# Rounding in three VectorE operations instead of four, before a bf16 product and before a transpose

## The reference

```python
def _layernorm(x, axis=-1, eps=1e-5):
    ...
    return (x - m) / jnp.sqrt(v + eps)

def _act_quant(x):
    scale = 127.0 / jnp.clip(jnp.max(jnp.abs(x), axis=-1, keepdims=True), 1e-05)
    xq = jnp.clip(jnp.round(x * scale), -128.0, 127.0) / scale
    return x + jax.lax.stop_gradient(xq - x)
def _bitlinear(x, w):
    return jnp.einsum('bsi,oi->bso', _act_quant(x), _weight_quant(w))

# feed-forward: HIDDEN = 1024, INNER = 4096
gate = jax.nn.silu(_bitlinear(x, w_gate))
up = _bitlinear(x, w_up)
return _bitlinear(gate * up, w_down)

# the layer
x = x + attention(_layernorm(x), ...)
x = x + feed_forward(_layernorm(x), w_gate, w_up, w_down)
```

## Time and profile before

| what | us |
|---|---|
| median of 2 runs | 8739.44 |
| lowest and highest run | 8737.64, 8741.25 |
| the profiled execution, its own time | 8731.81 |
| its span on core 1, the slowest | 8730.3 |
| spans of the 8 cores | 8703.8 to 8730.3 |
| VectorE busy | 5261.6 (60%) |
| TensorE busy | 4117.8 (47%) |
| ScalarE busy | 1586.2 (18%) |

### The profile page before, as it was taken

How to read it: one execution, slowest core, us unless ns; L and a number is a source line. 1 busy time by engine, 2 the same in 40 slices (tenths; PEclk the granted TensorE clock), 3 DMA queues, 4 the chain that set the end, 5 groups by cost and what they waited for, 6 DMA issues and landing times.

```text
span 8730.3 us, 121031 instructions; the slowest of 8 cores (8703.8 to 8730.3 us)
## 1 busy us (share of the span) xinstructions
PE 4117.8 (47%) x38438; PEld 2587.6 (30%) x38438; DVE 5261.6 (60%) x12636; ACT 1586.2 (18%) x2602; POOL 60.4 (1%) x102
## 2 busy tenths in 40 slices
PE   0015545555555546645455454555344353353453
PEld 0015522222222225522233232223233232232232
DVE  5666667777677666667677676664544435435434
ACT  0000023333333320013233232331000000000000
POOL 0000000000000000000000000000000000000000
PEclk9997778888888887778788787886666666565566
DMA  8641000000000001100000000002333333343343
GB/s 279 227 137 35 30 4 1 4 1 4 1 1 1 1 18 35 37 7 1 4 1 1 4 1 1 1 1 61 65 82 80 75 87 63 68 93 64 75 87 68
DMA packets 835921, 394.33 MB, mean 45 GB/s; under 512 B 803427, under 2 KB 803555, under 8 KB 829156
## 3 DMA queue, kind: packets, MB, share of 16 engines
q1 hardware_dynamic: 827044, 353.00, 17.1%
q0 software_dynamic: 8256, 33.58, 0.9%
HBM read 352.95 MB, written 33.55 MB: 44 GB/s over the span
## 4 chain that ended last, share of the span: by engine, by line
DVE 47%; PE 26%; issue 11%; DMA 7%; DVEq 7%; ACT 1%; SPq 0%; ACTq 0%; POOLq 0%; POOL 0%
DVE w_lo L771 15%; DVE w_hi L769 9%; PE pb_av L454 6%; PE pf_u L1189 2%; PE pf_d L1361 2%; PE pf_g L1184 2%; PE pf_d L1189 2%; PE pf_d L1184 2%; DMA f_wd<-wdq 2%; PE pb_s L736 2%; DVE ln_lo L471 2%; DVE ln_hi L469 2%; PE pb_o L840 1%; DVE f_guq L1334 1%; PE pb_q L840 1%
## 5 line engine op out<-in xcount | busy, mean ns | idle before, releaser
L759 ACT ACTIVATE w<-pb_s,cbias 128x512 f32<-128x512 f32 x2048 | 1297.4, 684 | 1532.9 <-PE pb_s L736 1519.9
L771 DVE TENSOR_TENSOR w_lo<-w,w_hi 128x512 bf16<-128x512 f32 x2048 | 1416.8, 692 | 159.1 <-issue 6.8
L769 DVE CAST w_hi<-w 128x512 bf16<-128x512 f32 x2048 | 874.8, 427 | 563.8 <-issue 357.1
L712 PE MATMUL pb_av<-vA,w_hi 128*128 128x129 bf16 x4096 | 516.5, 226 | 1142.3 <-DVEq L774 1142.1
L712 PEld LDWEIGHTS pb_av<-vA,w_hi 128*128 128x128 bf16 x4096 | 383.5, 100 | 1642.7 <-issue 1642.7
L1361 PE MATMUL pf_d<-f_guq,f_wd 128*128 128x256 bf16 x2048 | 291.9, 315 | 667.0 <-DVE f_guq L1334 560.6
L712 PE MATMUL pb_av<-vB,w_hi 128*128 128x129 bf16 x4096 | 517.1, 226 | 0.0
L736 PE MATMUL pb_s<-q_hi,h_hi 64*128 64x512 bf16 x2048 | 463.3, 412 | 102.7 <-ACT w L759 71.7
L716 PE MATMUL pb_av<-vA,w_lo 128*128 128x65 bf16 x4096 | 491.1, 198 | 0.0
L716 PE MATMUL pb_av<-vB,w_lo 128*128 128x65 bf16 x4096 | 489.4, 198 | 0.0
L736 PE MATMUL pb_s<-q_lo,h_hi 64*128 64x512 bf16 x2048 | 458.6, 407 | 0.0
(11 more groups left out here) (220 smaller groups left out, 6856.8 us busy)
## 6 DMA issues: line engine op xcount, KB each, us to landing
f_wg<-wgq SPq DMA_DIRECT2D x256, 256.0 KB, 3.2
f_wu<-wuq SPq DMA_DIRECT2D x256, 256.0 KB, 3.7
f_wd<-wdq SPq DMA_DIRECT2D x64, 1024.0 KB, 8.4
wraw<-wgT SPq DMA_DIRECT2D x16, 2048.0 KB, 10.2
wraw<-wuT SPq DMA_DIRECT2D x16, 2048.0 KB, 9.9
wraw<-wdT SPq DMA_DIRECT2D x64, 512.0 KB, 4.5
xa<-x_full SPq DMA_DIRECT2D x64, 512.0 KB, 3.5
x_tm<-x_full SPq DMA_DIRECT2D x16, 512.0 KB, 13.5
```

What stands on the lines that cost most here:

```text
L712: te.matmul(pav[:, pofs:pofs + 129], w_hi[:, wofs + st * 128:wofs + (st + 1) * 128], vb[:, rc * 132:rc * 132 + 129], start=(rc == 0 and st ...
L759: a_e.inc(sc.activation(w32[:, slot:slot + 512], pb_s[hidx][:, 0:512], AFT.Exp, bias=cbias[:, hidx:hidx + 1], scale=1.0 / 64))
L769: v.tensor_copy(w_hi[:, slot:slot + 512], w32[:, slot:slot + 512])
L771: v.tensor_tensor(w_lo[:, slot:slot + 512], w32[:, slot:slot + 512], w_hi[:, slot:slot + 512], ALU.subtract)
```

## The change

The result t g + (u + v) becomes u h + v with h = g + 1, kept in a new tensor `h_t` of one fp32 value per partition. Where g is 0, h is 1 and the result is u + v. Where g is -1, h is 0 and the result is v. This takes the addition and the DRAIN behind it out of both quantizations, and the last operation reads `f_u` and `f_v` (or `f_si` and `f_fb`) in place of `f_t` and `f_u` (or `f_gr` and `f_si`). At the start, one DRAIN and one 128x1 operation are added, and the semaphore `s_g` is raised by the new operation. `h_t` is declared before all large buffers but `x_tm`, so that what is declared behind it starts 32 bytes later.

```diff
--- before.py
+++ after.py
@@ -92,6 +92,7 @@
     onesb = sb("onesbs", [1, 128], BF16)
     eps_t = sb("eps_t", [128, 1], F32)
     g_t = sb("g_t", [128, 1], F32)
+    h_t = sb("h_t", [128, 1], F32)
     sc_t = sb("sc_t", [128, 8], F32)
     mkrow = sb("mkrow", [1, 32], F32)
     mh_row = sb("mh_row", [1, 512], F32)
@@ -147,7 +148,9 @@
         v.drain()
         v.tensor_sub(sc_t[:, 2:3], sc_t[:, 1:2], sc_t[:, 0:1])
         v.drain()
-        s_g.inc(v.tensor_scalar(g_t[:], sc_t[:, 2:3], 4.0, -1.0, ALU.mult, ALU.add))
+        v.tensor_scalar(g_t[:], sc_t[:, 2:3], 4.0, -1.0, ALU.mult, ALU.add)
+        v.drain()
+        s_g.inc(v.tensor_single_scalar(h_t[:], g_t[:], 1.0, ALU.add))
 
     with ExitStack() as wes:
         wsb = lambda n, s, d: wes.enter_context(nc.sbuf_tensor(n, s, d))
@@ -1071,10 +1074,8 @@
                     v.tensor_scalar(f_u[:], f_t[:], M23, -M23, ALU.add, ALU.add)
                     v.tensor_scalar(f_v[:], f_t[:], M52, -M52, ALU.add, ALU.add)
                     v.drain()
-                    v.tensor_add(f_u[:], f_u[:], f_v[:])
-                    v.drain()
                     v.scalar_tensor_tensor(f_xq[:, st2 * E:(st2 + 1) * E],
-                                           f_t[:], g_t[:, 0:1], f_u[:],
+                                           f_u[:], h_t[:, 0:1], f_v[:],
                                            ALU.mult, ALU.add)
                     v_fq.inc(v.drain())
 
@@ -1329,11 +1330,9 @@
                     v.tensor_scalar(f_si[:], f_gr[:], M23, -M23, ALU.add, ALU.add)
                     v.tensor_scalar(f_fb[:], f_gr[:], M52, -M52, ALU.add, ALU.add)
                     v.drain()
-                    v.tensor_add(f_si[:], f_si[:], f_fb[:])
-                    v.drain()
                     v_gq.inc(v.scalar_tensor_tensor(
-                        f_guq[:, oc * FSC:(oc + 1) * FSC], f_gr[:], g_t[:, 0:1],
-                        f_si[:], ALU.mult, ALU.add))
+                        f_guq[:, oc * FSC:(oc + 1) * FSC], f_si[:], h_t[:, 0:1],
+                        f_fb[:], ALU.mult, ALU.add))
                     v.drain()
 
             @blk.sync
```

## The result

The changed kernel took 8602.68 us at the median (8594.75 to 8628.27 us, 7 runs), the kernel before 8736.98 us beside it (8728.13 to 8741.92 us, 6 runs). The ratio is 0.9852 with a 95% interval of 0.9838 to 0.9865, which is 129 us less by the ratio and 134 us by the medians, where 149.7 us were forecast. Timed again beside nine more runs of before, it gave 0.9841 (0.9822 to 0.986). The forecast time was 8590 us in a range of 8568 to 8615 us.

What follows compares the result with a forecast made beforehand. No engine is full; the kernel is a row of stages where one engine works while another waits. Savings of 128.9 + 20.8 + 0 = 149.7 us from 8739.4 us give 8590 us, range 8568 to 8615 us.

Steps and rivals of the forecast that it cites:

- both loops are bare on the path: Feed-forward part: TensorE waits for both quantization loops in each of 8 chunks, 560.6 and 172.1 us, with nothing beside them.
- The terms: Savings counted: down quantization 128.9 us, activation quantization 20.8 us, start 0; together 149.7 us.
- `issue` gaps: Down quantization loop: the prediction is wrong if these idle gaps grow by what the removed addition took.
- What costs nothing: Last operation of the down quantization stays at 484 ns; the added start pair counts 0, up to 0.5 us uncovered.
- The size of the gain: 149.7 us, taken from core 1's span and then from the median; bounds 128.3 to 151.6 us.
- 8 us either way for the clock: Feed-forward part: TensorE's clock could change the time by up to about 1 us per chunk either way.
- Rival 1: Feed-forward part: TensorE's clock gives 3.1 us more per chunk, 25 us in all, time 8565 us or less; chance 3%.
- Rival 2: Down product: `f_wd` moved by 32 bytes loads 8% slower, adding 32 us, 8622 us; chance 6%.
- the margin of these loads: Down product: first two turns have their weights about 60 us before use, and about 44 us after the change.
- Rival 3: Attention: the shifted copy of line 769 slows from 427 to 692 ns, adding 543 us, 9133 us; chance 2%.
- Rival 4: Down product: something else holds it back, so the time stays at 8739 us; chance 4%.
- The flush behind an operation: Down quantization: DRAIN time lies beside the addition, pair 0.504 us; 159 ns on top would make 0.58 us, 150 us total.

Runs made afterwards that it cites:

- one pair more: Kernel before, with the down quantization's addition and its DRAIN made once more in each of 256 turns, into an unread buffer: 8868.19 us, ratio 1.0143.
- changed, once more: The changed kernel as it is, timed again beside more executions of before: 8597.61 us, ratio 0.9841.
- layout alone: Kernel before with only h_t declared and set at the start, so buffers behind g_t lie 32 bytes later: 8746.95 us, ratio 1.0006.
- no layout: Changed kernel with h kept in a free column of sc_t, so no buffer moves: 8604.28 us, ratio 0.9844.
- down quantization alone: Changed kernel with the addition and DRAIN put back in the activation quantization: 8624.01 us, ratio 0.9868.
- activation quantization alone: Changed kernel with the addition and DRAIN put back in the down quantization: 8728.01 us, ratio 0.9984.
- one DRAIN more: Changed kernel with a second DRAIN before line 1333 in each of 256 turns: 8598.71 us, ratio 0.9837.
- four blocks at a time: Changed kernel, down quantization on 1024 columns per turn: 8436.0 us; a second version also starts the first down matmuls beside it: 8393.78 us.

## Why the prediction was right

**That both loops are bare on the path** held in every test: for one pair more or less in the 256 turns of the down quantization TensorE's wait changed by 128 and 126 us, and for the activation quantization it fell by 19.8 us, with 14 to 16 us of the time when that edit stood alone.

**The terms.** Below are the stages, in us, as sums over the chunks and means over the 8 cores of the profiled executions, from the timelines. "Weights" ends with the start of the last rounding of a weight (line 269 of before), "first projection" with the start of the first maximum taken from `mh_row` (line 541), "attention" with the start of the last copy to `w_hi`. "Down quantization" is from the start of the copy of `f_sb` to the end of the last `f_guq`, "down product" from there to the start of the last copy of `f_do`, "to the next chunk" from there to the start of the copy of `f_fb` (7 of them, with the activation quantization in it), and "gate and up" from there to the copy of `f_sb`.

| kernel | weights | first projection | attention | gate and up | down quantization | down product | to the next chunk |
|---|---|---|---|---|---|---|---|
| before | 562.3 | 542.0 | 4815.7 | 1471.2 | 557.8 | 395.2 | 287.2 |
| changed | 563.4 | 545.2 | 4823.7 | 1470.5 | 431.9 | 391.6 | 268.6 |
| changed, once more | 557.9 | 545.0 | 4819.7 | 1472.7 | 432.1 | 397.3 | 268.9 |
| layout alone | 567.5 | 542.7 | 4818.7 | 1472.1 | 557.9 | 398.6 | 287.2 |
| no layout | 564.2 | 544.1 | 4819.1 | 1472.5 | 432.1 | 400.8 | 268.5 |
| down quantization alone | 568.3 | 542.9 | 4821.6 | 1475.3 | 429.1 | 399.0 | 287.4 |
| activation quantization alone | 564.6 | 542.7 | 4819.2 | 1473.2 | 558.0 | 392.0 | 268.5 |
| one DRAIN more | 561.8 | 543.5 | 4820.4 | 1476.0 | 442.0 | 393.1 | 268.7 |
| one pair more | 564.8 | 543.3 | 4814.4 | 1472.2 | 685.6 | 391.7 | 287.1 |

The down quantization lost 125.9 us where 128.9 us were counted. The missing 3 us are the `issue` gaps of the loop, which the prediction had named as a thing that could grow (4.0 us before, 7.0 us after). They are not chance: on all 8 cores of both profiles of the changed kernel and of the one without the layout they are 7.0 us. With the down quantization alone edited the same loop has 2.6 to 2.9 us of them, and its stage lost 128.7 us. What sets them isn't shown. The activation quantization lost 18.6 us in 7 chunks, 21.3 us in 8, where 20.8 us were counted. The first lies inside its bounds and the second 0.3 us above its upper one of 21.0 us, and together they are 147.2 us of the 149.7 us.

**What costs nothing** cost nothing that can be seen: line 1333 kept 484 ns, and the layout moved the time by 1.0006 (0.9997 to 1.0015). Gate and up and the down product changed by less than the same stage differs among kernels in which nothing of it was edited (1470.5 to 1476.0 us, 391.6 to 400.8 us).

**The size of the gain** was overstated, by 12 to 15 us for the slowest core and by 10 us for the mean over the cores, and the step that was off is the last one, where a saving read off one core's stages was taken whole from the median of the slowest core. The stages gave 147 us. The mean of the 8 spans fell by 140 us in the one comparison of the changed kernel that has both, and by 140 us without the layout. The slowest core fell by 134 us the first time and by 137 us in each of these two.

In the profiled executions the 7 us between 147 and 140 lie in stages that no edit touches. Against the profile of before, attention took 8.0 us more in the changed kernel, 4.0 us more in its second profile and 3.4 us more without the layout, and the first projection 3.2, 3.0 and 2.1 us more; weights and down product went both ways. Attention took 4814.4 to 4818.7 us in the three kernels whose loops weren't shortened, and 4818.3 to 4823.7 us in the eight profiles of shortened ones (4818.3 and 4822.1 us in the two with four blocks at a time). That looks like an effect of the edit on code in front of it, but each is one execution, that of before was itself a quick one (mean span 8719.2 us, where the comparisons had 8722.8 to 8727.5 us), and no run tests it: it stays open.

The first projection shows a reason for the rest on the slowest core. TensorE's granted clock in the first projection, for 300 us from 600 us on (us, busy us and instructions of PE, PEld, DVE, ACT, POOL, then the clock, the DMA share and GB/s), first before:

```profile
600.00:900.00 300.00, 184.01 (x2059) 165.92 (x2056) 186.82 (x580) 26.70 (x60) 0.00 (x0) 0.73 0.12 36
```

the changed kernel, core 1 and then core 2:

```profile
600.00:900.00 300.00, 190.26 (x1976) 171.18 (x1975) 180.48 (x560) 26.17 (x60) 0.00 (x0) 0.67 0.12 34
```

```profile
600.00:900.00 300.00, 185.69 (x2076) 168.21 (x2076) 186.38 (x577) 25.36 (x57) 0.00 (x0) 0.73 0.10 35
```

and the same kernel in its second profile, core 1 and then core 3:

```profile
600.00:900.00 300.00, 183.97 (x2064) 165.81 (x2062) 187.33 (x582) 26.28 (x58) 0.00 (x0) 0.73 0.12 36
```

```profile
600.00:900.00 300.00, 187.90 (x1976) 169.12 (x1976) 183.77 (x570) 24.03 (x54) 0.00 (x0) 0.67 0.12 34
```

The slow ones had a clock of 0.67, the others 0.73. It was on cores 0 and 1 in the one profile (554.0 and 553.6 us for the first projection) and on cores 2 and 3 in the other (548.5 and 552.6 us), with the same program and the same layout on all. In the kernel without the layout cores 2 and 3 had 0.70 (548.1 and 548.6 us). All other cores of all profiles took 540.6 to 546.1 us. On core 1 the first projection took 553.6 us that time, 541.4 us in the kernel before. That is 12 us of the profiled execution's 33 us short on core 1; its second half of the attention took 9 us more as well (4828.4 us for the whole attention after 4819.3 us), which I did not follow further. The time is the slowest core's, so such an event on one core is enough. The prediction counted 8 us either way for the clock, and only in the feed-forward part; the term belongs to every stage with TensorE in it. Whether the changed kernel meets the lower clock more often than the one before, or it was met by chance in its two profiles and in that without the layout, and not in that of before, stays open: it happens ahead of both quantizations, and the only instructions added ahead of it are a DRAIN and a 128x1 operation at the start, which the kernel with the layout alone has too (541.3 to 543.9 us).

**The rivals.** Rival 1 (a clock that gives 3.1 us per chunk) did not occur: gate and up changed by 0.7 us in 8 chunks. Rival 2 (slower loads of the down weights) did not occur: 8.1 us to landing in the changed kernel, 8.3 us with the layout alone, and 99.2 us of waits. By the Trainium skill, DMA: Bandwidth & Descriptors, How a descriptor splits into AXI transactions, the bytes in front of an uneven start are counted too. That account is of reads; for the written side, moved here by 32 bytes, no run shows such a cost. The prediction also set the margin of these loads too low: the DMA share was 0.01 from 6160 us on and the first down matmul of that chunk came at 6240 us, so they were there some 80 us before their use and not 60 us, which changes nothing. Rival 3 did not occur: 427 and 428 ns. Rival 4 fell with the first wait.

**The flush behind an operation**: the pair was 0.504 us from start to start for a 425 ns addition and its DRAIN, and one pair more or less moved the wait by 0.49 to 0.50 us (127.9 and 125.8 us in 256 turns). Set right for the `issue` gaps (4.1 us before, 3.4 us with the pair more and 7.0 us with the pair less, means over the cores), the stage changed by 0.502 and 0.503 us per turn. The removed DRAIN began 0.03 us after the addition and not about 0.1 us, and ended 0.03 us after it (medians of 256); nearly all of its 429 ns lay beside the addition, as the prediction concluded from the 0.51 us. The Trainium skill, VectorE: DVE Perf Modes, The DRAIN you can't avoid, would have it at 0.58 us, an estimate, if its 159 ns came on top; these runs do not agree with that reading.

## What to carry to other kernels

Where the waits say that an engine's whole loop stands in front of another's first instruction, price one instruction of it from start to start on the timeline and multiply: added or removed, the pair of the down quantization came out within 3% here. Then ask what the fixed part of each operation costs, since doing the loop on four blocks at a time was worth 167 us by the medians and 168.7 us in its stages, more than the 134 us of the removed operations. Take the saving as one of the mean over the cores, and expect the slowest core to show some microseconds less.

## What was not expected of the hardware

In the first projection TensorE's granted clock, as a mean over 300 us of the same loop, was 0.66 or 0.67 on two neighbouring cores in each of two executions of one program, where the other cores had 0.72 to 0.74, and on core 1 the stage took 12 us more than the 541 us of before. The `issue` gaps of the down quantization were 7.0 us on all cores in both profiles of the changed kernel, and 2.6 to 2.9 us for the same 256 turns in the kernel with only that loop edited. A second DRAIN directly behind the first costs 0.05 us, so most of the price of a DRAIN between two dependent operations is the waiting itself. And the first matmuls of the down product, run in groups of eight beside VectorE, all took 1.86 to 1.87 us on all 8 cores, 0.23 us for a matmul at a granted clock of 0.50 (core 1, 6185 to 6216 us), the lower of its two levels, where the blocks of 64 behind them took 8.8 to 10.0 us, 0.14 to 0.16 us each.
